# Expert layers with split F32R products, and four groups in a loop turn

## What is computed

```python
x = x + tanh(g_xattn[L]) * xattn(...)
x = x + tanh(g_ffn[L])   * ffn(layernorm(x))

# ffn, both layers: the two best of 8 experts, softmax of their logits as gates
combine = sum(one_hot(top_i, 8) * gates[..., None], axis=-2)
for e in range(8):
    h = act(x @ w1[e].T)          # layer 0: relu, 512 inner rows; layer 1: gelu, 64 inner rows
    y = h @ w2[e].T
    out = out + combine[..., e, None] * y
```

## Time and profile before

| | us |
|---|---|
| median of 3 runs | 4484.49 (4479.59 to 4485.52) |
| profiled execution | 4479.22 |
| its span | 4477.4 |

### The profile page before, as it was taken

The page is one execution under the profiler, slowest core; times in us unless marked ns, Lnnn a source line. Parts: engine busy times, 40 slices in busy tenths (PEclk is TensorE's granted clock), DMA queues, the critical chain, the costliest instruction groups (busy, mean ns, idle before and its releaser), DMA issues. The chain is left out here.

```text
span 4477.4 us, 76059 instructions
## 1 busy us (share of the span) xinstructions
PE 4194.4 (94%) x26651; PEld 2692.1 (60%) x26651; DVE 3394.0 (76%) x5328; ACT 3191.6 (71%) x5163; POOL 408.7 (9%) x348
## 2 busy tenths in 40 slices
PE   3999999999999999999978599999999999999995
PEld 2666666666666666666645366666666666666664
DVE  5878788787878888888742577777777777777775
ACT  3888888888888888888842367676766676766661
POOL 3111111111111111111100000000000000000000
PEclk9999999999999999999979699999999999999996
DMA  1000000000000000000011000000000000000000
GB/s 41 12 1 16 1 15 3 1 16 1 17 1 1 16 1 17 1 5 12 1 51 33 20 1 16 1 9 9 5 12 5 12 5 12 1 16 1 16 1 23
DMA packets 27290, 48.20 MB, mean 11 GB/s; under 512 B 9329, under 2 KB 18425, under 8 KB 24313
## 3 DMA queue, kind: packets, MB, share of 16 engines
q1 hardware_dynamic: 24824, 42.30, 2.9%
q10 hardware_dynamic: 2066, 0.69, 0.1%
HBM read 42.15 MB, written 0.82 MB: 10 GB/s over the span
## 5 line engine op out<-in xcount | busy, mean ns | idle before, releaser
L818 DVE TENSOR_TENSOR a_probs_lo<-a_probs 128x1024 fp32r<-128x1024 f32 x1764 | 2119.8, 1223 | 652.3 <-ACT a_probs L663 305.5
L659 ACT ACTIVATE a_probs<-scores_ps,a_c_bias,a_k_rstd 128x512 f32<-128x512 f32 x1892 | 1317.2, 776 | 35.3 <-PE scores_ps L1135 33.8
L1160 PE MATMUL out_ps<-a_probs_lo,a_v 128*128 128x512 f32 x3520 | 1134.5, 443 | 0.0
L1153 PE MATMUL out_ps<-a_probs,a_v 128*128 128x512 bf16 x3520 | 967.5, 390 | 38.1 <-DVE a_out_acc L831 27.8
L663 ACT ACTIVATE a_probs<-scores_ps,a_c_bias 128x1024 f32<-128x1024 f32 x818 | 870.3, 1112 | 114.5 <-PE scores_ps L1135 113.5
L1135 PE MATMUL scores_ps<-a_q_hi,a_k_hi 64*128 64x512 f32 x3528 | 793.0, 445 | 16.9 <-issue 9.1
L1160 PEld LDWEIGHTS out_ps<-a_probs_lo,a_v 128*128 128x128 f32 x3520 | 658.7, 188 | 219.9
L1135 PE MATMUL scores_ps<-a_q_lo,a_k_hi 64*128 64x512 f32 x3528 | 702.4, 393 | 0.0
L1135 PE MATMUL scores_ps<-a_q_hi,a_k_lo 64*128 64x512 f32 x3528 | 698.0, 390 | 0.0
L1153 PEld LDWEIGHTS out_ps<-a_probs,a_v 128*128 128x128 f16 x3520 | 273.5, 96 | 590.4 <-issue 221.9
L628 ACT ACTIVATE a_v<-proj_ps 128x256 f16<-128x256 f32 x456 | 175.5, 385 | 517.8 <-PE proj_ps L1070 517.6
(11 more groups left out here) (194 smaller groups left out, 3404.9 us busy)
## 6 DMA issues: line engine op xcount, KB each, us to landing
a_den<-a_inv_row SPq DMA_DIRECT2D x18, 1024.0 KB, 4.7
normed<-in_L_xattn_we_g SPq DMA_DIRECT2D x18, 256.0 KB, 2.7
a_wkv_raw<-in_L_xattn_wkv_g SPq DMA_DIRECT2D x18, 128.0 KB, 2.1
a_wo_raw<-in_L_xattn_wo_g SPq DMA_DIRECT2D x18, 128.0 KB, 2.1
m_w<-in_L_ffn_w1T SPq DMA_DIRECT2D x1, 2048.0 KB, 8.4
m_w<-in_L_ffn_w2T SPq DMA_DIRECT2D x1, 2048.0 KB, 12.8
a_wq_raw<-in_L_xattn_wq_g SPq DMA_DIRECT2D x18, 64.0 KB, 1.9
residual<-in_x SPq DMA_DIRECT2D x1, 512.0 KB, 4.0
```

The lines of the kernel that those rows point to most:

```text
L659: ins = nc.scalar.activation(probs[:, pb, e * 512:(e + 1) * 512], scores[:, b, e * 512:(e + 1) * 512], ACT.Exp, bias=cbias[:, tile:tile + ...
L818: nc.vector.tensor_tensor(plow[:, idx % NPL, :], probs[:, idx % NB, :], p_hi[:, idx % NB], ALU.subtract).then_inc(plo_ready, 1)
L1153: nc.tensor.matmul(outs[:, e * 512:(e + 1) * 512], v16[:, c % 2, t, e, :], p_hi[:, idx % NB, e * 512:(e + 1) * 512], start=t == 0, stop=False)
L1160: nc.tensor.matmul(outs[:, e * 512:(e + 1) * 512], v32[:, c % 2, t, e, :], plow[:, idx % NPL, e * 512:(e + 1) * 512], start=False, stop=t ...
```

## The change

- Semaphores come from `alloc_semaphore`, and those of the first attention layer are cleared by GpSimd before the first expert layer's block.
- The attention loops hold four groups in a turn, on every engine: 2 turns and 1 jump back a layer.
- Gates are laid out by expert, transposed by TensorE, copied, written to DRAM (`comb_row`) and read back with one row spread over the partitions.
- L = 0: weights are loaded expert by expert into two buffers, and the router waits for its own weights only. Weights, normed rows and hidden rows are split in a high part and the rest; `hidden(k)` is 6 F32R products (three for each half of the rows), Relu writes the high part, and VectorE makes the low one from PSUM. `project(k)` takes w2 as the weights and gives transposed outputs, 6 F32R products of 512 columns, summed over the four chunks of an expert in one of three banks. `project(k)` stands behind `hidden(k+1)` on TensorE. VectorE multiplies the transposed output by the spread gate row (`gated_half`) and sums over experts (`add_half`), and at the end the sum is transposed back and added to X.
- L = 1: all four chunks of hidden rows are made first; VectorE multiplies each by the gates of its two experts, and one PSUM sum over all chunks gives the outputs, which are added to X once. The output leaves in two halves.

```diff
-                with sp.Fori(0, NG // 2) as two:
-                    for odd in range(2):
-                        g = two * 2 + odd
+                with sp.Fori(0, NG // 4) as four:
+                    for sub in range(4):
+                        g = four * 4 + sub
...
+        def save_combine(sp):
+            sp.wait_ge(ct_read, ONCE)
+            sp.dma_start(comb_row.rearrange("e (t p) -> (e t) p", p=P), combT[:, :]).then_inc(cr_out, 16)
+            sp.wait_ge(cr_out, 16 * ONCE)
...
+            nc.clear_and_free_semaphores(B["used"])
...
+                    sp.dma_start(wg[:, :], A[NAME + "gateT"]).then_inc(w_in, 16)
+                    weights(0)
+                    weights(1)
+                    save_combine(sp)
+                    gate_rows(0)
+                    gate_rows(1)
+                    for e in range(2, NE):
+                        weights(e)
+                        gate_rows(e)
...
+                    split_weights(0)
+                    act.wait_ge(zt_done, ONCE)
+                    nc.scalar.activation(lnT[:, :], zt_ps, ACT.Copy).then_inc(zt_read, 1)
+                    nc.scalar.activation(x_hi[:, :], zt_ps, ACT.Copy).then_inc(xh_done, 1)
+                    for k in range(FC):
                         act.wait_ge(h_done, k + 1)
...
+                        if k >= NHB:
+                            act.wait_ge(h_used, k - NHB + 1)
+                        nc.scalar.activation(h_hi[:, k % NHB, :], scores[:, k % 2, :], ACT.Relu).then_inc(hh_done, 1)
...
+                    top_two(dve, step)
+                    hidden_low(0)
+                    combine(dve, step)
+                    for k in range(1, FC):
+                        hidden_low(k)
+                        e, j = k // JE, k % JE
+                        if e and j == 0:
+                            gated_half(e - 1, 0)
+                            gated_half(e - 1, 1)
+                        if e >= 2 and j == 1:
+                            add_half(e - 1, 0)
+                            add_half(e - 1, 1)
+                        if j == 2 and e + 1 < NE:
+                            weight_lows(e + 1)
...
+                    def hidden(k):
+                        e, j = k // JE, k % JE
+                        if j == 0:
+                            pe.wait_ge(wl_done, 2 * e + 2)
+                        if k >= 2:
+                            pe.wait_ge(hl_done, k - 1)
+                        w = slice(j * P, (j + 1) * P)
+                        for c in range(2):
+                            at = slice(c * 512, (c + 1) * 512)
+                            o = scores[:, k % 2, at]
+                            nc.tensor.matmul(o, w1h[:, e % 2, w], x_hi[:, at], start=True, stop=False)
+                            nc.tensor.matmul(o, w1l[:, e % 2, w], x_hi[:, at], start=False, stop=False)
+                            last = nc.tensor.matmul(o, w1h[:, e % 2, w], x_lo[:, at], start=False, stop=True)
+                        last.then_inc(h_done, 1)
+
+                    def project(k):
+                        e, j = k // JE, k % JE
+                        pe.wait_ge(hl_done, k + 1)
...
+                            if j == 0 and 2 * e + c >= 3:
+                                pe.wait_ge(y_mixed, 2 * e + c - 2)
...
+                    hidden(0)
+                    for k in range(FC):
+                        if k + 1 < FC:
+                            hidden(k + 1)
+                        if k == 1:
+                            turn_combine(pe)
+                        project(k)
...
+                    save_combine(sp)
+                    for c in range(FC):
+                        for i in range(2):
+                            sp.dma_start(spread[i * FH:(i + 1) * FH, c, :],
+                                         comb_row[2 * c + i:2 * c + i + 1, :].partition_broadcast(FH)).then_inc(g_all[c], 16)
...
+                    for k in range(FC):
+                        dve.wait_ge(gelu_done, k + 1)
+                        dve.wait_ge(g_all[k], g_base[k] + 32)
+                        nc.vector.tensor_tensor(hid[:, k, :], hid[:, k, :], spread[:, k, :], ALU.mult).then_inc(hg_done, 1)
...
+                    for k in range(FC):
+                        pe.wait_ge(hg_done, k + 1)
+                        for t in range(QT):
+                            last = nc.tensor.matmul(outs[:, t * P:(t + 1) * P], hid[:, k, t * P:(t + 1) * P], w2[:, k, :],
+                                                    start=k == 0 and t % 4 == 0, stop=k == FC - 1, skip_group_check=True)
```

More of the change, by code:

```diff
@@ L77, in sem @@
         def sem(name):
-            return ctx.enter_context(nc.semaphore(name))
+            return nc.alloc_semaphore(name=name)
         X = sb("residual", [P, QT, D])
@@ L152, in flamingo @@
         moe_sems = {}
+        used_sems = []
         for L in range(2):
@@ L218, in attention_layer @@
     NAME = "L%d_xattn_" % L
+    used = []
     def sem(name):
         only = ONLY.get(name)
-        return sem_("a%d_%s" % (L, name)) if only is None or only == L else None
+        if only is not None and only != L:
+            return None
+        used.append(sem_("a%d_%s" % (L, name)))
+        return used[-1]
     scope = ExitStack()
@@ L610, in _ @@
                     k_rstd(0, k)
-                with pool.Fori(0, NG // 2) as two:
-                    for odd in range(2):
-                        g = two * 2 + odd
+                with pool.Fori(0, NG // 4) as four:
+                    for sub in range(4):
+                        g = four * 4 + sub
                         for i in range(NPR):
@@ L749, in _ @@
                 read_kv(0, HEAD)
-                with act.Fori(0, NG // 2) as two:
-                    for odd in range(2):
-                        g = two * 2 + odd
+                with act.Fori(0, NG // 4) as four:
+                    for sub in range(4):
+                        g = four * 4 + sub
                         k0, s0 = g * NI, g * NS
@@ L996, in _ @@
                 k_var(0, HEAD)
-                with dve.Fori(0, NG // 2) as two:
-                    for odd in range(2):
-                        g = two * 2 + odd
+                with dve.Fori(0, NG // 4) as four:
+                    for sub in range(4):
+                        g = four * 4 + sub
                         k0, s0 = g * NI, g * NS
@@ L1181, in _ @@
                     score(0, 0, 0, n2)
-                with pe.Fori(0, NG // 2) as two:
-                    for odd in range(2):
-                        g = two * 2 + odd
+                with pe.Fori(0, NG // 4) as four:
+                    for sub in range(4):
+                        g = four * 4 + sub
                         k0, s0 = g * NI, g * NS
@@ L1289, in moe_layer @@
     FC = NE * FH // P
-    FE = FH // P if L == 0 else 1
-    KH = P if L == 0 else FH
+    JE = FC // NE if L == 0 else 1
     NAME = "L%d_ffn_" % L
@@ L1308, in sb @@
             return sb_("m%d_%s" % (L, name), shape, dt, scope)
-        w1 = sb("w1", [P, NE * FH])
-        w2 = sb("w2", [P, FC, D])
         wg = sb("wg", [P, NE])
-        hid = sb("hidden", [P, 4 if L == 0 else 1, NQ])
         logit = sb("logit", [P, QT, NE])
@@ L1319, in moe_layer @@
         one = sb("one_hot", [P, 2, QT, NE])
-        comb = sb("combine", [P, QT, NE])
+        comb = sb("combine", [P, NE, QT])
+        combT = sb("combine_T", [NE * QT, P])
+        comb_row = nc.dram_tensor("m%d_combine_row" % L, (NE, NQ), F32).ap()
         w_in, var, rs, z_ready = (sem_both(s) for s in ("w_in", "var", "rstd", "z_ready"))
@@ new lines, in moe_layer @@
+        cb_ready, ct_done, ct_read, cr_out = (sem_both(s) for s in ("comb_ready", "combT_done", "combT_read", "comb_out"))
+        g_in = [sem_both("gate_in%d" % i) for i in range(2)]
+        step_s, h_done = (sem(s) for s in ("step", "h_done"))
+        zt_ps = scores[:, 0, :]
+        def save_combine(sp):
+            sp.wait_ge(ct_read, ONCE)
+            sp.dma_start(comb_row.rearrange("e (t p) -> (e t) p", p=P), combT[:, :]).then_inc(cr_out, 16)
+            sp.wait_ge(cr_out, 16 * ONCE)
@@ new lines, in router, with turn_combine, top_two @@
+        def router(pe):
+            for t in range(QT):
+                last = nc.tensor.matmul(proj[:, t * NE:(t + 1) * NE], lnT[:, t * P:(t + 1) * P], wg[:, :],
+                                        start=True, stop=True, skip_group_check=True)
+            last.then_inc(lg_done, 1)
+        def turn_combine(pe):
+            pe.wait_ge(cb_ready, ONCE)
+            nc.tensor.transpose(proj[0:QT * NE, 0:P], comb[:, :, :].rearrange("p e t -> p (e t)"), ident[:, :]).then_inc(ct_done, 1)
+        def top_two(dve, step):
+            dve.wait_ge(lg_done, ONCE)
+            step(nc.vector.tensor_copy(logit[:, :, :], proj[:, 0:QT * NE].rearrange("p (t e) -> p t e", e=NE)))
+            for t in range(QT):
+                nc.vector.max(top[:, t, :], logit[:, t, :]).then_inc(step_s, 1)
+            step.n += QT
```

(20 more changed lines are left out.)

303 lines of the change are left out of this document (181 added, 122 removed).

## The result

| | before | after |
|---|---|---|
| median, us | 4485.01 (4479.59 to 4485.96, 4 runs) | 4427.38 (4427.15 to 4428.44, 4 runs) |
| profiled execution, us | 4479.22 | 4427.17 |
| its span, us | 4477.4 | 4425.4 |

The ratio is 0.9876 with an interval of 0.9864 to 0.9888: 57.6 us or 1.2% faster. 4429.7 was forecast.

What follows compares the result with a forecast made beforehand. TensorE was taken as the bound; savings of 33.7 (L0), 14.0 (L1) and 7.1 us (loops), 54.8 in all, take 4479.22 to 4424.4 profiled, with 5.3 a median of 4429.7. Likeliest case 4425 to 4436; range 4419 to 4447.

Steps and rivals of the forecast that it cites:

- The 5.3 that I added for the median: Whole kernel: median of three runs before lay 5.27 us above the profiled execution, so the forecast was moved up by that.
- L0's experts: First expert layer's loop: TensorE makes 48 F32R products at 0.23 us, 11.0 us an expert in place of 15.39.
- The other engines: First expert layer: VectorE about 9.5 and ScalarE 5.3 us an expert, both under 11.0; hand-overs fit by 0.2 us.
- rival (a): First expert layer: VectorE and hand-overs set the pace, 12.5 us an expert, 10.5 us more in all, 4440.2; chance 0.17.
- L0's start: First expert layer's head: router starts at 2312.5 without waiting for all weights; pace doubles about 2321.8; first expert ends 2331.8.
- L0's end: First expert layer's tail: 5.0 us follow the last product, before 1.1; VectorE ends at 2413.8 against 2447.5; layer saves 33.7.
- Clearing semaphores: GpSimd ahead of the first expert layer's block: costs 0, up to 3 us if the clear takes twice as long.
- L1's expert layer: Second expert layer: gates, broadcasts and restart at the low clock end at 4463.4, saving 14.0 us.
- Rival (c): Second expert layer: broadcasts come late and TensorE stays slow, 2.5 + 3 + 1.5 us less saved, 4436.7; chance 0.10.
- Four groups in a turn: Attention loops: one jump back a layer in place of three, 2 x 2.6 + 2 x 0.95 = 7.1 us saved.
- The slower rival (e): First expert layer: F32R products take 0.427 us, 20.5 us an expert, making the time 4504; chance 0.03.
- rival (f): First expert layer: gates by DRAM come later than the output products need them, 4434; chance 0.02.

Runs made afterwards that it cites:

- two_products: Changed kernel without the lo-hi product of each triple in the first expert layer, 32 products an expert in place of 48; 4419.41 us in one run.
- vector_more: Changed kernel with one more VectorE addition of 128x512, which nobody reads, for each chunk of the first expert layer; 4436.85 us in one run.
- before_four: Kernel before with four attention groups in a turn as its only edit; median 4474.47 us, ratio to before 0.9981.
- flat: Changed kernel with no loop in attention, eight groups written out, so no jump back; median 4422.35 us, ratio to before 0.9860.
- two_groups: Changed kernel with two attention groups in a turn again, new expert layers kept; median 4432.98 us, ratio to before 0.9887.

## Why the prediction was right, point by point

The forecast was 4429.7 and the median 4427.38, inside the likeliest case's own range. The sum was made against the profiled execution, where it gave 4424.4 and the trace gave 4427.17, 2.8 more. Expert layers brought 1.9 more than forecast and attention 4.7 less. The 5.3 that I added for the median wasn't there: the profiled execution after lies at its median, the one before lay under its own. So that the forecast came within 2.3 us of the median is in part luck: attention's 4.7 less was made good by the 5.3 and by the 1.9.

**L0's experts: right.** 10.99 an expert against 11.0, the product at 0.229 against 0.23 from the earlier trace rows, and 33.89 saved against 33.7. The row of the same width and kind was the right one to price by; the 256-column row would have made it 11.3.

**The other engines: right, the slack too.** VectorE is busy for 8.50 of 10.99, where I had 9.0 and 0.5 of waits, so 1.5 free; two_products and vector_more put what it could still take at 1.3, and rival (a) did not come. The 0.2 by which the hand-overs fitted is another quantity, how much later a low could be in one chunk. It stands up as well: the low is done 0.23 to 0.29 us before the product that needs it, and some 0.06 of that is the hand-over itself (in two_products the low ends at 2362.20 + 1.22 and the product starts at 2363.48).

**L0's start: right.** Timeline of TensorE after, against the earlier trace rows:

```profile
2308.52 3.58 PE L1342 MATMUL proj_ps<-m_wg,normed_T 128*128 128x8 f32 x16 [1.11 <-ACT normed_T L1436]
...
2317.31 0.72 PE L1545 MATMUL out_ps<-m_hidden_hi,m_w_hi 128*128 128x512 f32 x1
2317.87 0.40 PE L1546 MATMUL out_ps<-m_hidden_hi,m_w_lo 128*128 128x512 f32 x1
```

The wait of 5.23 us for weights is gone; what remains is 1.11 for the copy on ScalarE. From the layer's start at 2298.85 the router starts 9.67 in, where 2312.5 - 2302.84 = 9.66 was forecast, and the pace doubles at 2317.87, 19.0 in, as forecast.

**L0's end: right.** Timeline after:

```profile
2403.65 0.50 PE L1545 MATMUL spare_ps<-m_hidden_hi,m_w_hi 128*128 128x512 f32 x1 [0.98 <-DVE m_hidden_lo L1464]
...
2408.91 0.69 DVE L1509 TENSOR_TENSOR residual<-scores_ps,residual 128x512 f32<-128x512 f32 x1 [0.22 <-PE scores_ps L1561]
```

VectorE ends at 2409.6, 110.75 into the layer, against 110.96 forecast. In the last chunk there is no further hidden product to cover the low, and TensorE waits 0.98 us, the hand-over that every other chunk hides.

**Clearing semaphores: right, 0.** VectorE's wait for GpSimd's rstd is 1.8 us, the longest of its kind, before and after.

**L1's expert layer: the sum right to 1.75 us, by sizes that offset each other.** From the layer's start:

| step | forecast | measured |
|---|---|---|
| gates copied | 21.8 | 20.3 |
| store of the gates, its own time | 1.4 | 1.8 |
| first broadcast landed, from its issue | 3.5 | 4.7 |
| a further 512 KB | 1.4 | 2.1 to 2.3 |
| TensorE restarts | 28.1 | 28.15 |
| clock rises, from the restart | 8.8 | 4.8 |
| last product | 39.4 | 37.9 |
| end | 43.1 | 41.4 |

The step that failed is the price of the broadcasts: I had taken it from a_den, 1024 KB in one DMA, at 2.7 us a MB. Here it is 4.4 us a MB in eight DMAs of 256 KB, about 240 GB/s. Rival (c) named it and priced it at 3 us. Beside their number, these broadcasts differ from a_den in that each fills 64 partitions and not 128; which of the two makes them slower was not tried. What paid for it is the clock, which rose 4 us sooner than the pattern of L0's start had it, and the gates, which were copied 1.5 us sooner. The 8.8 itself isn't what the rows say: the earlier trace rows have 2325.95 - 2316.60 = 9.35 from the restart, which would have made the forecast some 0.3 us longer. The store of 32 KB took 1.8 us; the 8 KB row says 1.4. The Trainium skill ("DMA: Bandwidth & Descriptors", Anatomy of one DMA) gives about 2.0 of fixed cost for DMAs that GpSimd issues, and this store, issued by SP, lies under it.

**Four groups in a turn: the mechanism right, the size mis-sized for the second layer.** Forecast 7.1; the timed runs give 8.2 in the old kernel (before_four) and 4432.98 - 4427.38 = 5.6 in the new, though the latter compares different chips. In the two profiled executions it was 2.4. L0 gave 4.0 for 5.2: its jumps brought what was forecast, but one more group than before had 1.5 us of extra time (last section). The 2.6 a jump was in part lucky, since each of the two averages that it was taken from held one group with this 1.5. L1 gave nothing for 1.9, since its one jump cost 3.2; that group got 2.15 us longer, which by the prediction's own sign, 1 us a group, is wrong. The term "2 x 0.95" took a jump's price as fixed, from three jumps with stands of up to 1.7 us, and a jump behind which the clock falls costs three times that.

The rest of L1's +1.63 is at its head, where VectorE waited 3.9 us instead of 2.4 for the context to land; in flat, two_groups and before_four it was 2.3, 3.0 and 3.1, so this is no price of the change that the traces could show. That the gain is there at all, which by the compare-and-branch price of the Trainium skill ("Advanced Engine Details and Errata", Control Flow Timing) it wouldn't be, is shown by before_four and two_groups: 1.8 to 2.0 us for each jump against 0.1. The same skill's statement that a jump out of the fetched window stalls ("Runtime: NRT & Kernel Launch", Instruction fetch mechanics) is what the stands look like, though no run shows the fetch itself.

**The slower rival (e) and rival (f)** had nothing in them: 0.229 us a product, and no wait of VectorE for gates in L0.

## What to carry to other kernels

Price a product by the row of the same width and type in the same kernel, and then ask which engine is next and by how much: taking work away from the bound (two_products) and adding work to its neighbour (vector_more) measure that in two runs. Keep two kinds of slack apart: how much more work the neighbour can take (1.3 us an expert here), and how much later one of its results may come (0.2 us a chunk). A loop's jump back cost 1.8 to 2.0 us here on the engine that bounds, so where few turns are made it is worth unrolling. Several small broadcasts are not priced by one large one, and where the tail of a kernel waits for them, TensorE can come back at half its clock, as it did here after 6.43 us of idle time.

## What the runs showed of the hardware that I had not expected

Not only jumps: a group without one also has two lengths. In flat, which has no jump, groups of the first layer take 268.94 to 268.97 or 270.42 to 270.47, in turn. In the middle of each, TensorE waits for VectorE; timeline of flat:

```profile
1585.93 0.40 PE L1159 MATMUL out_ps<-a_probs,a_v 128*128 128x512 bf16 x1 [1.47 <-DVE a_out_acc L837]
```

Windows of flat, first this wait and what follows 2 us later, then the same place one group earlier:

```profile
1584.00:1586.00 2.00, 0.53 (x5) 0.21 (x2) 1.95 (x3) 2.00 (x5) 0.00 (x0) 1.00 0.00 0
1588.00:1590.00 2.00, 2.00 (x14) 1.09 (x16) 0.00 (x0) 1.20 (x2) 0.00 (x0) 0.50 0.00 0
1315.00:1317.00 2.00, 0.53 (x5) 0.20 (x3) 1.90 (x3) 2.00 (x5) 0.00 (x0) 1.00 0.00 0
1319.00:1321.00 2.00, 2.00 (x22) 1.11 (x19) 0.14 (x1) 1.45 (x2) 0.00 (x0) 1.00 0.04 8
```

TensorE is busy for 0.53 of 2 us both times. After the one pause the clock falls to 0.50 and the group gets 1.5 us longer, after the other it doesn't. The seven groups between the second store and the ninth of this layer, in each of before, after and flat, bear it out: all nine of 270.4 to 270.5 or 273.05 to 273.1 us have a fall to about 0.50 some 125 us behind the store, and none of the twelve others has one there. With that taken out, the jump of this layer costs 2.5 to 2.8 us each time. What decides whether the clock falls behind one and the same pause, no run here shows. So a difference of 1.5 us between two traces of this kernel may be that alone. Whether this makes the 6 us by which runs of the kernel before differ among themselves was not tried.
